# Routing made group by group during the attention, token rows scattered into two tables, and both tables gathered by the experts

## The reference

```
x   = x + cross_attention(layernorm(x), ctx)      # 16 heads of 16
h   = layernorm(x)                                # (N = 4096, D = 256)
scores = softmax(h @ wg); gates, idx = top_k(scores, 2); gates /= sum(gates)
# the place of each (token, choice) in its expert: all first choices in token order, then all second choices
loc  = cumsum(masks, 0) - 1 + offsets             # offsets of choice 2 = counts of choice 1
keep = loc < C                                    # C = 1280 rows for each of the 8 experts
y    = silu(rows @ fc1_w.T + fc1_b) @ fc2_w + fc2_b   # for each expert, hidden width 1024
out  = x + layernorm(h + sum(gates * y)) * gamma + beta
```

## Time and profile before

| | |
|---|---|
| median of 3 runs | 844.66 us (844.61 to 844.91) |
| the profiled execution: own time, span | 846.77 us, 845.0 us |
| mean granted clock of TensorE | 0.903 of full speed |
| busy: PE, DVE, POOL, ACT | 703.3, 583.0, 433.6, 395.0 us |
| attention, routing, experts, tail, about | 0 to 297, 297 to 360, 360 to 804, 804 to 845 us |

### The profile page before, as it was taken

The page is one execution under the profiler, slowest core; times in us unless marked ns, Lnnn a source line. Parts: engine busy times, 40 slices in busy tenths (PEclk is TensorE's granted clock), DMA queues, the critical chain, the costliest instruction groups (busy, mean ns, idle before and its releaser), DMA issues.

```text
span 845.0 us, 17103 instructions
## 1 busy us (share of the span) xinstructions
PE 703.3 (83%) x5635; PEld 665.6 (79%) x5637; DVE 583.0 (69%) x1177; ACT 395.0 (47%) x899; POOL 433.6 (51%) x480
## 2 busy tenths in 40 slices
PE   3599999999999912299999996999979999999600
PEld 2578998999889811299999996999969999999500
DVE  3868888788887689556556667768656566764268
ACT  1225555555555421235444455556445444653265
POOL 3614545536444354653555466656656545532456
PEclk9569999999999965589999997999989999999855
DMA  9300111011101132023434436445443443332375
GB/s 292 122 1 27 38 39 37 26 39 39 38 26 38 41 123 56 26 66 76 102 49 91 93 53 148 73 95 104 113 104 49 91 95 51 53 46 26 35 229 174
DMA packets 55328, 63.86 MB, mean 76 GB/s; under 512 B 9296, under 2 KB 50512, under 8 KB 55120
## 3 DMA queue, kind: packets, MB, share of 16 engines
q0 software_dynamic: 15360, 21.31, 15.5%
q1 hardware_dynamic: 34784, 40.96, 14.9%
q10 hardware_dynamic: 5104, 0.44, 0.5%
HBM read 38.96 MB, written 23.72 MB: 74 GB/s over the span
## 4 chain that ended last, share of the span: by engine, by line
PE 78%; DVE 10%; issue 5%; DMA 3%; POOL 2%; ACT 1%; SPq 0%; DVEq 0%; POOLq 0%; ACTq 0%
PE banks L745 17%; PE banks L747 17%; PE banks L746 17%; PE banks L856 9%; PE banks L843 5%; PE banks L831 5%; PE banks L953 2%; PE banks L909 2%; POOL oh_id L523 2%; DMA sum_rows<-y_sb,slot_ids 1%; DVE z L1397 1%; PE banks L869 1%; DMA wv_sb<-in_wvT 1%; PE banks L779 1%; PE banks L899 1%
## 5 line engine op out<-in xcount | busy, mean ns | idle before, releaser
L501 POOL DMA_INDIRECT sum_rows<-y_sb,slot_ids x80 | 129.3, 1617 | 188.9 <-ACT y_sb L694 158.6
L704 ACT ACTIVATE hraw<-banks,b_now 128x256 f32<-128x256 f32 x320 | 132.3, 474 | 104.7 <-PE banks L747 93.3
L745 PE MATMUL banks<-xT_hi,w_hi 128*128 128x256 f32 x560 | 163.4, 292 | 3.5 <-issue 3.5
L747 PE MATMUL banks<-xT_hi,w_lo 128*128 128x256 f32 x560 | 160.4, 286 | 0.3 <-issue 0.3
L746 PE MATMUL banks<-xT_lo,w_hi 128*128 128x256 f32 x560 | 160.3, 286 | 0.0
L745 PE MATMUL banks<-w_hi,h_hi 128*128 128x256 f32 x528 | 148.9, 282 | 3.0 <-issue 3.0
L746 PE MATMUL banks<-w_lo,h_hi 128*128 128x256 f32 x528 | 148.6, 281 | 0.0
L747 PE MATMUL banks<-w_hi,h_lo 128*128 128x256 f32 x528 | 148.4, 281 | 0.0
L1341 DVE CAST h_hi<-hraw 128x512 fp32r<-128x512 f32 x160 | 74.8, 468 | 66.4 <-ACT hraw L704 64.6
L1343 DVE TENSOR_TENSOR h_lo<-hraw,h_hi 128x512 fp32r<-128x512 f32 x160 | 113.0, 706 | 5.5
L746 PEld LDWEIGHTS banks<-xT_lo,w_hi 128*128 128x128 f32 x560 | 108.3, 193 | 3.7 <-issue 3.7
(11 more groups left out here) (193 smaller groups left out, 1470.0 us busy)
## 6 DMA issues: line engine op xcount, KB each, us to landing
w1raw<-in_w1T SPq DMA_DIRECT2D x8, 1024.0 KB
w2raw<-in_w SPq DMA_DIRECT2D x8, 1024.0 KB
xn_rows<-xn SPq DMA_DIRECT2D x32, 128.0 KB, 1.8
sum_rows<-xn SPq DMA_DIRECT2D x32, 128.0 KB, 1.8
out<-z SPq DMA_DIRECT2D x16, 256.0 KB, 2.2
res<-sum_rows SPq DMA_DIRECT2D x7, 512.0 KB, 7.8
X<-in_x SPq DMA_DIRECT2D x2, 1280.0 KB, 14.2
xg<-xn_rows,slot_ids POOLq DMA_INDIRECT x80
```

Source lines behind the costliest of these rows:

```text
L501: g.indirect_dma_start(sum_rows, bass.IndirectOffsetOnAxis(ap=slot_ids[:, st, 1, q:q + 1], axis=0), y_sb[:, u, q, :], None, bounds_check=N ...
L704: a.activation(hraw[:, j // 2, j % 2, :], banks[:, j // 2, (j % 2) * 256:(j % 2 + 1) * 256], ACT.Silu, bias=b1_now[:, (c // SPE) % 2, j:j ...
L745: t_.matmul(o, a_hi, b_hi, start=first, stop=False)
L747: return t_.matmul(o, a_lo, b_hi, start=False, stop=last)
```

## The change

- **Routing in the attention.** The 32 tiles form 15 groups: three of 4 tiles, eight of 2, four of 1. For a group of tiles a to b-1, DVE's step b+3 picks both choices (11 small instructions, `pick_a` to `pick_f`, laid between its other work), PE counts them (2 matmuls), and DVE reads the counts and makes row numbers (`read_counts`, b-a+5 instructions). DVE makes the gates in the next step (6 instructions, `gate_a` to `gate_f`), for the last four groups in the same step. ACT takes two exponentials for each group.
- **Two tables.** Each row of 264 numbers (row, 8 gates, and 8 copies of its token number, so 272 in all) is scattered by POOL with indirect transfers to `first_rows` at expert * 1280 + its place among first choices, and to `second_rows` in the same way: two transfers for each tile, 64 in all, from a ring of 12 rows of tiles. They start at step 8. SP stores only `sum_rows`, one transfer for each tile.
- **Clearing.** Both tables (10,240 rows of 1,088 bytes each) are first written with zeros by two transfers that ACT issues at its step 1 (`zero_tables`). POOL waits for them before it scatters.
- **Loops.** All engines' attention steps are written out.
- **Experts.** A super-tile is gathered with four indirect transfers in place of two: from the first table, and then, when that has landed, from the second; numbers out of bounds leave a row as it is. The row to add to is read from the gathered row. DVE, not POOL, splits expert 0's low parts and adds `beta`.
- Gone: `top_two`, the one-hot matrices with their 64 matmuls, `slot_ids`.

```
+            def zero_tables():
+                act.wait_ge(sem("empty_made"), 1)
+                act.wait_ge(load_x[3], 16)
+                for rows in (first_rows, second_rows):
+                    act.dma_start(rows[0:NE * CAP, :].rearrange("(p n) w -> p n w", p=P),
+                                  row_ring[:, 8:9, :].to_broadcast([P, NE * CAP // P, W])).then_inc(tables_zeroed, 16)
...
+                if t == 1:
+                    zero_tables()
                 probs_transposed(0)
...
+            def read_counts(k):
+                a, b = GROUPS[k]
+                dve.wait_ge(sem("counted"), k + 1)
+                for j in range(b - a):
+                    last()
+                    routed(v.tensor_tensor(next_row[:, a + j + 1, :], next_row[:, a + j, :],
+                                           banks[:, CB, TOTALS + RE * j:TOTALS + RE * (j + 1)], ALU.add))
...
+            def scatter_rows(t):
...
+                pool.wait_ge(sem("gated"), k + 1)
+                pool.wait_ge(sem("ids_written"), t + 1)
+                pool.wait_ge(sem("xn2_made"), t + 1)
+                pool.wait_ge(sem("row_no_made"), k + 1)
+                for r, rows in enumerate((first_rows, second_rows)):
+                    wait(pool, row_out[r][(t - 1) % 2], 16 * ((t - 1) // 2 + 1))
+                    g.indirect_dma_start(rows, bass.IndirectOffsetOnAxis(ap=row_no[:, t, r:r + 1], axis=0),
+                                         ring_row(t), None, bounds_check=NE * CAP - 1, oob_is_err=False)\
+                        .then_inc(row_out[r][t % 2], 16)
...
+            def gather_second(st):
+                if within(st, NST):
+                    u = st % SPE
+                    pool.wait_ge(gathered_first[u], 32 * (st // SPE + 1))
+                    for q in range(2):
+                        g.indirect_dma_start(xg[:, st % XR, q, :], None, second_rows,
+                                             bass.IndirectOffsetOnAxis(ap=slot_second[:, st, q:q + 1], axis=0),
+                                             bounds_check=NE * CAP + 4 * P - 1, oob_is_err=False).then_inc(gathered[u], 16)
...
+            gather_first(0)
+            gather_first(1)
+            pool.wait_ge(sem("ids_made"), 2)
+            for n in range(2):
+                pool.wait_ge(row_out[1][n], 16 * NT // 2)
+            gather_second(0)
+            pool.wait_ge(sem("trash_zeroed"), 16)
+            for st in range(2, AHEAD + 1):
+                gather_first(st)
+                gather_second(st - 1)
```

More of the change, by code:

```diff
@@ L259, in attention_steps @@
                         spread(2 * i + u + 1)
[L260 to L265, removed]
             step(PAIRS + 1, 0)
@@ L326, in store_xn @@
             def store_xn(i, u):
[L327 to L331, removed]
+                t = 2 * i + u - 3
+                if within(t, NT):
+                    sp.wait_ge(sem("xn2_made"), t + 1)
+                    wait(sp, sum_out[t % 4], 16 * (t // 4))
+                    sp.dma_start(sum_rows[t * P:(t + 1) * P, :], ring_row(t)[:, 0:D]).then_inc(sum_out[t % 4], 16)
             attention_steps(sp, store_xn)
@@ L911, in step @@
                     m.then_inc(sem("logits_done"), 1)
+                if group_of_step(t) is not None:
+                    count(group_of_step(t))
                 weigh_values(3)
@@ L1138, in step @@
             def step(i, u):
                 t = 2 * i + u
+                picked, gated = group_of_step(t), group_of_step(t - 1)
+                if gated is not None and gated >= AT_ONCE:
+                    gated = None
                 if within(t - 2, NT):
@@ L1149, in step @@
                                     ALU.mult).then_inc(sem("vals_made"), 1)
+                if picked is not None:
+                    pick_a(picked)
+                if gated is not None:
+                    gate_a(gated)
                 def shift(f):
@@ L1167, in step @@
                 shift(0)
+                if picked is not None:
+                    pick_b(picked)
+                if gated is not None:
+                    gate_b(gated)
                 if within(t - 2, NT):
@@ L1172, in step @@
                         .then_inc(sem("valsT_lo_made"), 1)
+                if picked is not None:
+                    pick_c(picked)
+                if gated is not None:
+                    gate_c(gated)
                 shift(1)
+                if picked is not None:
+                    pick_d(picked)
+                    pick_e(picked)
+                if gated is not None:
+                    gate_d(gated)
                 if u == 1:
                     queries_lo(i + 1)
+                if picked is not None:
+                    pick_f(picked)
                 if within(t - 2, NT):
@@ L1185, in step @@
                     dve.wait_ge(sem("st1_made"), 2 * i + 6)
+                if gated is not None:
+                    gate_e(gated)
                 if u == 0:
@@ L1188, in step @@
                     first_lo(i + 1)
+                if gated is not None:
+                    gate_f(gated)
                 if within(t - 2, NT):
@@ L1305, in _, with over_slots @@
-            then(v.scalar_tensor_tensor(above[:], empty[:], 0.0, trash[:].rearrange("p s q -> p (s q)"),
-                                        ALU.is_equal, ALU.mult))
-            v.scalar_tensor_tensor(slot_ids[:, :, 1, :], sid[:].rearrange(pair, q=2), -float(P),
-                                   above[:].rearrange(pair, q=2), ALU.add, ALU.add).then_inc(sem("ids_made"), 1)
+            step(PAIRS + 1, 1)
+            n_first, n_second = next_row[:, NT, 0:NE], next_row[:, NT, NE:RE]
+            def over_slots(x2):
+                return x2.unsqueeze(2).to_broadcast([P, NE, 2 * SPE])
@@ new lines, in _ @@
+            last()
+            routed(v.tensor_tensor(src[:], src[:], is_empty[:], ALU.max))
+            last()
+            v.scalar_tensor_tensor(slot_second[:].rearrange("p s q -> p (s q)"), not_second[:].rearrange(flat), float(SKIP),
+                                   src[:].rearrange(flat), ALU.mult, ALU.add).then_inc(sem("ids_made"), 1)
+            for n in range(4):
+                dve.wait_ge(sem("w_hi_made"), n + 1)
+                hi, lo, raw = w_parts(0, n)
+                v.tensor_tensor(lo, raw, hi.bitcast(f32), ALU.subtract).then_inc(sem("w_lo_made"), 1)
```

502 lines of the change are left out of this document (293 added, 209 removed).

## The result

The changed kernel takes 881.91 us (median of 4 runs, 880.82 to 883.00); the kernel before took 844.78 beside it. The ratio is 1.0431, with an interval from 1.0401 to 1.0460: slower by 37 us. The prediction was 910, with 840 to 939 as its range. The profiled execution took 880.83 us, with a span of 879.1, which is 34.1 more than the span before.

A forecast was written before the change was run, and what follows sets the result against it. PE was taken to set the attention's pace by a narrow margin, with routing a 63 us hole in its work. 844.7 + 56 (hold) + 32 (DVE) + 2 (experts) - 25 (hole) = 909.7, 910 us; range 840 to 939.

The forecast's parts named there:

- The hold, 56 us: At attention step 1, the sum's first term: issuing the zeros holds ACT 60 us, 4 covered; bounds 0, 51 and 83.
- SP was free 10 us before the end: Loads of X at the start: SP's issue returned 10 us before landing; so zeros taking 70 us hold ACT for 60.
- its step 2: Profile sign at the zeros: ACT's queue holds two issues some 60 us, PE idle; a first issue under 5 us refutes it.
- Rival A's condition: At the zeros: the issue does not hold ACT, the queue takes both transfers as commands; whole 56 us saved, chance 0.15.
- DVE in the attention, 32 us: Eleven groups' small routing instructions stretch attention pairs and wait for POOL's port: 32 us, between 24 and 44.
- The wait for POOL: In the attention, two-operand DVE instructions stand until POOL's current one ends: 1.8 us a group, 20 in all.
- The hole, -25: Routing between attention and experts: the gap before the first fc1 shrinks by 25 us; other ends 16 and 32.
- steps 32 and 33: End of the attention: the last groups' small DVE instructions make the last residual come 3.5 us later.
- a step back: POOL's scatters in the attention: waits for an earlier tile's landing lie a step back; POOL's term there is nothing.
- POOL and the experts, +2: POOL adds nothing in the attention; in the experts near-empty super-tiles leave it behind, 2 us, 0 to 8.

The follow-up runs named there:

- experiments 1: The changed kernel with SP instead of ACT issuing the two clearing transfers: 856.35 us, ratio 1.0126.
- 3: The kernel before plus only the clearing, two transfers issued by ACT into two unused tables: 867.12 us, ratio 1.026.
- 4: The kernel before plus 24 small DVE instructions, all of one SBUF operand, in each of eleven pairs of attention steps: 863.25 us, ratio 1.0216.
- experiment 5: The kernel before plus 24 small DVE instructions in each of eleven pairs of attention steps, 13 reading two SBUF operands: 884.95 us, ratio 1.0428.
- Experiment 2: The changed kernel with ACT clearing the tables in eight transfers of 2,560 rows in place of two of 10,240: 905.44 us, ratio 1.0719.
- experiment 12: The changed kernel, SP clearing, two gate instructions in place of six, early gathers reordered, later ones paused until the first fc1 is done: 849.06 us, ratio 1.0033.
- 10: The changed kernel with SP clearing and two gate instructions in place of six, run again on a third chip: 870.05 us.

## Why the prediction came out as it did

**The sign and the terms: right, the sizes of two of them not.** The zeros hold ACT (experiments 1 and 3), DVE's instructions stretch the pairs (4, 5), and what the hole gives back does not pay for both. That 881.9 lies 28 below 910 is nearly all the first term.

**The hold, 56 us: the term that was mis-sized.** It measured 25.0. The failing step is "SP was free 10 us before the end", carried over as "less the last 10, ACT is held for 60". The traffic was right: 70 us predicted, 70.5 from the first issue to the last landing. But the ten microseconds were what was left of loads of 1.31 MB; what is left when an issue returns is here one to two transfers, and with two transfers of 35 us each that is 40 us. The prediction named a first issue under 5 us as what refutes its step 2, and by that sign it is refuted in part: all of the hold is the second issue's. Rival A's condition was therefore half true: the first large issue costs 0.58 us, and by that row one table alone would have held ACT for next to nothing, which was not tried. The Trainium skill's sentence that I used (Perfetto Trace Analysis, DMA Instruction — HWDGE), that the issuer is occupied until the descriptors are generated, stood in the right direction for the second issue. What the prediction drew from it, that this issue cannot be free, the first issue contradicts: 10,240 rows in 0.58 us. Experiment 2, with equal rows and bytes and 54 us in place of 30, shows that the number of transfers matters too.

**DVE in the attention, 32 us: measured 30.4,** by a sum whose parts are partly others, so that it comes this near is in part luck. Bare instructions are 1.71 us a pair (predicted 2.1). The wait for POOL is as the prediction read it, to the end of POOL's current instruction (230.07 after 230.03). Its size is 1.45 us a group in experiment 5, 15.9 in all (predicted 1.8 and 20). In the changed kernel itself it is 1.3 us a group on average, 1.0 with two tiles and 2.1 with four; experiment 5 puts its two-operand instructions in other places beside POOL, which may be the difference and was not tested. Not foreseen: a dip of TensorE's granted clock from 1.00 to 0.62 (2.4 GHz towards 1.2) after PE had been busy 2.38 of 4 us before step 8, worth 1.6 us.

**The hole, -25: measured -20.6,** of which steps 32 and 33 cost 4.2 (predicted 3.5). What the prediction did not have are POOL's two waits for landings, 3.28 and 2.91 us, and two scatters of 1.9 us in place of 1.0, together 8 us. They are not all lost: DVE is done with tile 31 14.0 us after the last residual (predicted 15.8), and the remaining overlap was not split. The prediction put "a step back" for these waits, which holds in the attention (one wait of 1.0 us between 134 and 343); at the end, where steps are as short as the scatters, it does not. The two scatters at 363.31 and 364.62 landed after 5.52 and 4.57 us, in place of 2.5, while SP's load of the biases (1,024 KB, issued at 363.07) was under way.

**POOL and the experts, +2: measured -0.7** on the chip of the result.

The terms together: 31.0 us less hold, 1.6 less DVE, 2.7 less in the experts, and against them 4.4 less gain; that is 31 below 910, and the medians lie 3 us further apart than the two profiled spans (37.1 against 34.1). That gives the 28 by which 881.9 differs from 910.

**What stays open.** Why PE starves on two chips of three (or at two times of three), and why only in the changed kernel: experiment 5 ran on the second chip with 484.7 us after its first fc1, no stall. Its trace differs in the gathers too: after the code packet (400.13) POOL issues six, the last at 409.05 and the next at 432.05, where the changed kernel issues a dozen 1.3 us apart. The six traces time the stall with the code packet and the gathers, and in experiment 12, with a pause, it is absent; that the code waits behind the gathers in a queue is argued from this, not shown. The missing run is 10 and 12 beside each other on a chip that stalls.

## What to carry to other kernels

Before a large transfer is issued, ask which engine issues it and who waits for that engine: here the same bytes cost 25 us on ACT and nothing on SP. If the issuer must be a busy engine, prefer few large transfers: here two held it 30 us and eight 54.

Price a small instruction by where it stands: 0.07 us between independent ones, 0.21 in a chain, and 0.1 more on average for two SBUF operands beside a busy POOL; its own duration, 0.16, is none of these.

Where a hole ends in a burst of gathers, gather first what the next matmul needs. A pause behind it is worth a try where PE stalls with nothing to wait for.

## What the runs showed of the hardware

- The first transfer of 10,880 KB held its issuing engine 0.6 us, the second 28 to 30 us, on ACT and on SP alike; eight of 2,720 KB held it 54.
- A small DVE instruction with two SBUF operands that began while a POOL instruction ran ended with it (230.07 after 230.03, 239.12 after 239.06); of 35 that took over 0.3 us, two of them with one operand, 32 did.
- Zeros repeated from one row of each SBUF partition to HBM went at 350 GB/s, and PE beside them was busy 38.68 of 40 us, as without them.
- On two chips PE issued one matmul mostly each 0.7 to 1.4 us for 14 to 17 us in the first super-tiles; the same kernel took 856.4 us on one chip and 873.9 on another, while the kernel before differed by under 1 us.
- Scatters of 128 rows landed in 2.5 us in the median, and in 4.6 to 5.8 beside a load of 1,024 KB.
